# Decoder layer on one core: VectorE takes a unit of exponentials in chunks 1 and 16 too, the accumulators are summed inside a unit, and their transposes are spread over three chunks

## The reference: what is computed

```python
x = layernorm(x + distance_attention(x, U))         # softmax(-squared distances) @ x
q, k, v = x @ Wq + bq, ctx @ Wk + bk, ctx @ Wv + bv # 16 heads of 8
attn = softmax(q k^T / sqrt(8)) ; out = attn @ v    # 1024 x 6404 for each of 16 heads
x = layernorm(x + out @ Wo + bo)
x = layernorm(x + ffn(x))                           # gated, with fake-quantised weights and inputs
```

## Time and profile before

| | |
|---|---|
| median of 3 runs | 824.02 us (822.88 to 824.13) |
| profiled execution | 824.79 us, of which the span from first to last instruction is 823.1 us |
| busy share of the span | ACT 89%, PE 86%, DVE 74%, POOL 21% |
| cross attention | from about 103 us to about 776 us of the span |
| one phase | 83.6 us |

### The profile page before, as it was taken

One profiled execution on the slowest core, in us unless ns is written; L12 is line 12 of the kernel. 1 busy time (PEld: TensorE's weight loads), 2 busy tenths in 40 slices (PEclk: granted clock), 3 DMA queues, 4 the chain that ended last, 5 costly groups with the idle time before them and its releaser, 6 DMA issues.

```text
span 823.1 us, 36628 instructions
## 1 busy us (share of the span) xinstructions
PE 705.3 (86%) x15084; PEld 316.5 (38%) x15084; DVE 609.9 (74%) x1712; ACT 733.5 (89%) x650; POOL 170.7 (21%) x304
## 2 busy tenths in 40 slices
PE   6996679999999999998999898999999999989841
PEld 3444424443444344434443444334433443344321
DVE  3519756886888688858886888778877886788666
ACT  2436788999999999999999999999999999999741
POOL 2501511221222122212221222122211221122100
PEclk9999989999999999999999999999999999999975
DMA  3303521111111111111111111111111111111000
GB/s 106 83 22 115 169 86 48 44 41 41 43 38 37 43 46 36 37 44 44 40 35 42 45 40 35 41 45 41 35 40 46 41 35 40 41 36 35 5 1 25
DMA packets 36607, 38.36 MB, mean 47 GB/s; under 512 B 8430, under 2 KB 35088, under 8 KB 36512
## 3 DMA queue, kind: packets, MB, share of 16 engines
q1 hardware_dynamic: 35644, 36.59, 15.5%
q10 hardware_dynamic: 868, 0.48, 0.2%
HBM read 30.15 MB, written 6.42 MB: 44 GB/s over the span
## 4 chain that ended last, share of the span: by engine, by line
ACT 54%; issue 26%; PE 9%; DVE 4%; SPq 3%; DMA 1%; ACTq 1%; POOL 1%; POOLq 0%; DVEq 0%
ACT probs L714 53%; SPq L291 2%; PE ps L1224 2%; PE ps L1210 2%; PE ps L1325 1%; DMA k_parts_dram<-k_parts 1%; ACTq L727 1%; DMA q_parts_dram<-q_parts 1%; DVE stats L780 1%; POOL k_parts L545 1%; PE ps L1173 1%; DVE probs L1104 0%; PE ps L1152 0%; SPq L312 0%; ACTq L712 0%
## 5 line engine op out<-in xcount | busy, mean ns | idle before, releaser
L714 ACT ACTIVATE probs<-ps 128x1536 f32<-128x1536 f32 (+1 forms) x536 | 669.5, 1393 | 6.4 <-PE ps L1295 6.4
L1325 PE MATMUL ps<-probs,v_op 64*9 64x512 f32 (+1 forms) x8256 | 524.7, 499 | 3.8 <-DMA k_op<-k_parts_dram 3.8
L1295 PE MATMUL ps<-q_op,k_op 59*32 59x512 bf16 x6432 | 335.4, 383 | 64.6 <-ACT probs L714 61.7
L1295 PEld LDWEIGHTS ps<-q_op,k_op 59*32 59x32 bf16 x6432 | 103.6, 90 | 349.7 <-issue 258.7
L964 DVE TENSOR_SCALAR e_t<-ps 128x256 f32<-128x256 f32 x240 | 90.7, 419 | 146.9 <-PE ps L1295 146.9
L1325 PEld LDWEIGHTS ps<-probs,v_op 64*9 64x9 f32 x8256 | 172.4, 87 | 66.6 <-issue 10.1
L592 POOL TENSOR_SCALAR e_pow<-e_t 128x512 int32<-128x512 int16 x120 | 74.4, 620 | 356.4 <-DVE e_t L964 356.4
L585 POOL COPY v_op<-v_all 128x108 f32<-128x108 f32 x136 | 64.3, 473 | 175.1 <-PE ps L1325 174.4
L992 DVE SCALAR_TENSOR_TENSOR e_f<-e_f,e_pow 128x256 f32<-128x256 f32 x240 | 98.6, 449 | 0.0
L986 DVE SCALAR_TENSOR_TENSOR e_f<-e_u,e_f 128x256 f32<-128x256 f32 x240 | 90.4, 418 | 0.0
L981 DVE SCALAR_TENSOR_TENSOR e_u<-e_f 128x256 f32<-128x256 f32 x240 | 90.2, 417 | 0.2
(11 more groups left out here) (179 smaller groups left out, 262.8 us busy)
## 6 DMA issues: line engine op xcount, KB each, us to landing
k_op<-k_parts_dram SPq DMA_DIRECT2D x544, 36.0 KB
k_parts_dram<-k_parts SPq DMA_DIRECT2D x17, 288.0 KB, 3.1
k_op<-k_parts_dram SPq DMA_DIRECT2D x272, 12.0 KB
ctx_nat<-in_ctx_dram SPq DMA_DIRECT2D x16, 192.0 KB, 2.9
q_op<-q_parts_dram SPq DMA_DIRECT2D x32, 48.0 KB
q_parts_dram<-q_parts SPq DMA_DIRECT2D x2, 384.0 KB, 4.3
x_nat<-in_x_dram SPq DMA_DIRECT2D x1, 512.0 KB, 3.7
o_t<-att_rows SPq DMA_DIRECT2D x28, 16.0 KB
```

The costliest lines, as they stand in the source:

```text
L714: act.activation(probs[:, b % NP].rearrange("p u t -> p (u t)")[:, 0:columns], ps[:, bank:bank + BU, :].rearrange("p u t -> p (u t)")[:, 0 ...
L1295: return pe.matmul(ps[a:a + P // G, bank, :], k_op[W2 * r:W2 * r + KR, kslot, i, P * j + a:P * j + a + P // G], q_op[W2 * r:W2 * r + KR, q ...
L1325: last = pe.matmul(ps[32 * k:32 * k + DH + 1, ACC[h], a:b], v_op[W2 * h:W2 * h + W2, slot, j, (DH + 1) * k:(DH + 1) * (k + 1)], probs[W2 * ...
```

## The change

ScalarE's instruction for block s = 2 gets 1024 columns in chunks 1 and 16 as well, and VectorE and GpSimd do a unit there: 17 units in a phase for 15. `power` is cut in two, `factors` (the two stages of the polynomial that need no power of two) and `power` (the last two). `add_acc` stands between `factors` and `power` of chunk 0, where it stood between `take` and `power`. The four instructions that turn and normalise the accumulators stood behind the unit of chunk 0; now `turn_acc` stands behind the unit of chunk 1, `normalise_acc` behind that of chunk 2, `turn_rows` behind that of chunk 3. On TensorE the values of chunk 16 move one step later in chunk 0, from s = 0, 1, 2 to s = 1, 2, 3, with a wait for the unit of chunk 16 in front of the last; and step s = 1 of chunk 0 waits until the unit of chunk 16 has been taken out of its bank.

```diff
-E_UNITS = NC - 2
+E_UNITS = NC
...
-            return ph * E_UNITS + max(c - 1, 0) + 1
+            return ph * E_UNITS + c + 1
...
-                    if c != 1 and c < NC - 1:
-                        powers(ph, c)
+                    powers(ph, c)
...
                 for s in range(BPC, 2 * BPC):
-                    exponentials(f + s, f + (s + 1 + AHEAD))
-                with act.Fori(0, E_UNITS // 2) as r:
+                    exponentials(f + s, f + (s + 1 + AHEAD), shared(s - BPC))
+                with act.Fori(0, (NC - 3) // 2) as r:
...
                 for s in range((NC - 1) * BPC, BPP):
-                    exponentials(f + s, f + (s + 1 + AHEAD))
+                    exponentials(f + s, f + (s + 1 + AHEAD), shared(s - (NC - 1) * BPC))
...
             for ph in range(PHASES):
-                take(ph, 0)
-                if ph:
-                    add_acc(ph - 1)
-                power(ph, 0)
-                if ph:
-                    turn_acc()
...
-                for c in range(2, NC - 1):
+                for c in range(NC):
                     take(ph, c)
+                    factors(ph, c)
+                    if ph and c == 0:
+                        add_acc(ph - 1)
                     power(ph, c)
+                    if ph and c == 1:
+                        turn_acc()
+                    if ph and c == 2:
+                        normalise_acc()
+                    if ph and c == 3:
+                        turn_rows(ph)
...
+                    if s == 1 and c == 0 and ph:
+
+                        pe.wait_ge(e_step, E_STEPS * (e_count(ph - 1, NC - 1) - 1) + E_TAKEN)
...
                     if c == 0:
-                        if s < CT:
-                            values(slot, f - LAST_BPC, s, True, count=2 if s == 1 else 1)
+                        if s == 3:
+                            pe.wait_ge(e_probs, 2 * e_count(ph - 1, NC - 1))
+                        if s:
+                            values(slot, f - LAST_BPC, s - 1, True, count=2 if s == 2 else 1)
...
             for j in range(CT):
                 pe.wait_ge(probs_ready, BLOCKS + min(j + 1, 2))
+                if j == CT - 1:
+                    pe.wait_ge(e_probs, 2 * E_UNITS * PHASES)
```

More of the change, by code:

```diff
@@ L972, in take, with factors @@
                                              ).then_inc(e_step, 1)
-            def power(ph, c):
-                block = ph * BPP + c * BPC + E_BLOCK
+            def factors(ph, c):
                 done = E_STEPS * (e_count(ph, c) - 1)
-                a, b, d, e = EXP2
+                a, d = EXP2[0], EXP2[2]
                 for n, cols in enumerate(halves):
@@ L988, in power @@
                                              ).then_inc(e_step, 1)
+            def power(ph, c):
+                block = ph * BPP + c * BPC + E_BLOCK
+                done = E_STEPS * (e_count(ph, c) - 1)
+                b, e = EXP2[1], EXP2[3]
                 for n, cols in enumerate(halves):
@@ L1004, in turn_acc, with normalise_acc @@
                 acc_chain.step(dve.reciprocal(att_rden[:], acc_t[:, :, DH]))
+            def normalise_acc():
                 acc_chain.step(dve.tensor_tensor(
@@ L1008, in turn_acc, with turn_rows @@
                             [list(att_rden[:].ap[0]), [1, HQ // R], [0, DH]]), ALU.mult))
+            def turn_rows(ph):
+                if ph > 1:
+                    dve.wait_ge(o_written, 16 * G * (ph - 1))
+                dve.transpose(att_rows[:], acc_t[:].rearrange("p n d -> p (n d)")).then_inc(att_ready, 1)
             for ph in range(PHASES):
-                take(ph, 0)
-                if ph:
-                    add_acc(ph - 1)
-                power(ph, 0)
-                if ph:
-                    turn_acc()
-                    if ph > 1:
-                        dve.wait_ge(o_written, 16 * G * (ph - 1))
-                    dve.transpose(att_rows[:], acc_t[:].rearrange("p n d -> p (n d)")).then_inc(att_ready, 1)
-                for c in range(2, NC - 1):
+                for c in range(NC):
                     take(ph, c)
+                    factors(ph, c)
+                    if ph and c == 0:
+                        add_acc(ph - 1)
                     power(ph, c)
+                    if ph and c == 1:
[4 more added lines that the diff above has]
+                        turn_rows(ph)
             dve.wait_ge(x1_bo_ready, 1)
```

## The result

The changed kernel takes **835.06 us**, the median of 6 runs (830.86 to 841.76), beside 824.08 us for the kernel before (6 runs, 822.88 to 826.18): a ratio of 1.013, 95% interval 1.0084 to 1.0175. Forecast were 826.1 us and a range up to 828.4. The profiled execution took 836.24 us with a span of 834.5. So the kernel is slower, and by some 9 us more than I had worked out.

A forecast was written before the change was run, and what follows sets the result against it. ScalarE was taken to set the pace. Seven changes of phase at +0.16 us, +1.1, plus 0.95 in the tail gave 2.05 us on 824.02: 826.1 us, range 822.6 to 828.4.

The forecast's parts named there:

- a unit given away is worth 0.43 us: ScalarE's shortened block: 0.915 us against 1.345 for a full one; two units give 0.86 us per change of phase.
- the new unit of chunk 16 lies too close ahead of that of chunk 0: VectorE at a change of phase: units three blocks, 3.6 us, apart, while one takes 4.02 to 4.09 us.
- 1.02 us late in chunk 1: ScalarE's exponentials of s = 3 end at 12.46 instead of 11.44 us; bounds 0.78 to 1.13.
- The walk: Step-by-step timing of a change of phase from VectorE's chunk 16 unit; add_acc done at 8.1 to 8.2 us.
- No wait in chunk 0's steps: Expected sign: chunk 0's new waits cost nothing, being covered by VectorE's own lateness.
- TensorE's wait at some 1.4 us: Expected sign: TensorE's first values in chunk 1 wait for add_acc, once in each phase from 1 on, seven times.
- -0.86 + 1.02 = +0.16 ... Seven: +1.1 us: Net per change of phase, ScalarE's gain against its lateness, bounds -0.08 to +0.27; over seven, -0.6 to +1.9 us.
- no term has: Stated way to be wrong: the tail's granted clock falls at another time, which was given no size.
- my rivals: ScalarE keeps pace, 819.0 us (8%); half absorbed, 822.5 (12%); VectorE lengthened more, 828.0 or 830.0 (15%); free tail unit, 825.1.
- the slower one: Rival, 15%: GpSimd's copy holds VectorE 0.28 us in both units ahead of add_acc, 830.0 us; in one, 828.0.
- Spread as they are, they cost nothing: Turning instructions make chunk 2's take some 0.4 us late, within the 0.5 us TensorE's scores are ahead of ScalarE.
- The tail: Behind the last block: VectorE's new unit delays the residual add and statistics, everything behind 0.95 us later (0.9 to 1.1).

The follow-up runs named there:

- filled kernel: Changed kernel with the scores of chunk 1, s = 1 written three times over instead of once, to fill TensorE's idle stretch: 828.39 us, ratio 1.0044.
- Order alone: Kernel before with the two stages of factors put ahead of add_acc in chunk 0, no unit added: 834.62 us, ratio 1.0101.
- Order repaired, units kept: Changed kernel with add_acc put back between take and factors of chunk 0, added units kept: 827.74 us, ratio 1.0035.
- `add_acc` last: Changed kernel with add_acc two stages later, behind all of chunk 0's unit: 840.95 us, ratio 1.0191.
- one extra writing: Kernel before with factors ahead of add_acc and the scores of chunk 1, s = 1 written twice: 832.92 us, ratio 1.0086.
- order-only kernels: Kernel before with factors ahead of add_acc, no unit added: 834.62 us; with chunk 1, s = 1 scores written twice 832.92, three times 827.09.

## Why the prediction was wrong

**What held.** ScalarE sets the pace; a unit given away is worth 0.43 us; the new unit of chunk 16 lies too close ahead of that of chunk 0; the wait for `acc_step` takes the place of the gain, seven times; ScalarE comes out 1.02 us late in chunk 1. The walk gave that 1.02 and the profile shows it to the hundredth, in every phase without a fall and in all of the filled kernel; that it is the hundredth is luck, since my own bounds were 0.78 to 1.13 and single steps were off by 0.1. "No wait in chunk 0's steps" held, and so did the direction. I had put TensorE's wait at some 1.4 us from the moment the values could begin; the profile counts 1.11, from the end of the scores.

**The step that failed** is the size given to the change of phase: "-0.86 + 1.02 = +0.16 ... Seven: +1.1 us". It priced the wait by its length. A wait of TensorE has a second price, put at nothing there: behind it the granted clock may fall to one half, and then the scores that ScalarE is waiting for are the very ones that come at half speed. The rows of before do not show it; TensorE waits 0.40 and 0.73 us for ScalarE in the same steps there, and the clock stays. Measured: 1.69 us in chunk 1 at each fall, 1.55 us by the whole phase, four falls in each of two profiles, 6.2 us. With it, 826.1 becomes 832.3, and 833.2 with the smaller terms below. The last 1.9 us of the measured median are not accounted for; start-up, tail and perhaps the number of falls differ between executions. I named the granted clock only for the tail, as what "no term has", and did not carry the thought to the seven places where my own walk had TensorE standing idle. None of my rivals had it either: the slower one, held copies on VectorE at up to 830.0, named another mechanism, and the units back to back took 4.09 us each, as in my terms.

**Smaller terms.** "Spread as they are, they cost nothing" was off by 0.13 us in chunk 3, 0.9 us over seven phases where no fall covers it. I had chunk 2's take 0.4 late, and it is: unit 1 ends, the transpose and the reciprocal follow, and the take starts at 373.96 behind scores that end at 373.51. What I took for a cover of 0.5 us seems to have been a little less. Whether the turning or the late unit 1 is to blame was not told apart in this kernel. The tail was 0.82 us for 0.95. Without falls the sum would have been 7 x 0.30 + 0.82 = 2.9 us for my 2.05, which is 827.0 and inside the range. The filled kernel, which is that case, came out 4.4 us over the kernel before, so even there 1.5 us are without an account.

**The shares.** Order alone, with no unit added: +10.7 us. The whole change: +11.0. Order repaired, units kept: +3.8. The shares of units and order do not add up to the whole, because in both kernels falls of the clock do most of the damage. The part of the change that can pay is the unit in chunk 1, whose neighbours lie a full chunk away; the one in chunk 16 gives 0.43 to ScalarE and takes about a microsecond from it.

## What to carry to other kernels

Price a new wait of TensorE twice: by its length, and by what follows if the granted clock falls behind it, at the full-speed and half-speed lengths of the work that comes next; and do so most of all where that work feeds the engine that sets the pace. If the same matmuls take different times in different repetitions of a loop, look at the clock before anything else, and test it by filling the gap with useless work: a kernel that gets faster by computing more has named its cause. And where work is shared out to an engine with room on average, look at the distance between neighbouring pieces, not at the average.

## What the runs showed of the hardware

- An idle stretch of TensorE of 0.56 us ahead of a group of matmuls, at the end of 4.00 us in which it was busy for 2.31, was followed by half the clock in seven of seven places. The kernel before, busy for 2.87 of 4.00 us at the same place with idle stretches of 0.40 and 0.73 us, had no fall. With `add_acc` last it was busy for 1.14 of 4.00 and the clock fell in only two of seven; with one extra writing the last stretch was 0.13 us and it fell in four. So I can't give a rule for it, and the falls' beat of their own, above, may be part of the reason. The Trainium skill, TensorE: Matmul & The Clock Gate, the section "HAM oscillation — how this bites in real kernels", describes long waits for DMA that send the array back to half speed in every tile; here a wait of about half a microsecond for VectorE, on top of the waits that were there, did it.
- A fall costs ScalarE 1.1 to 1.7 us in chunk 1: 7.09 for 5.65 us in the order-only kernels, 7.65 for 5.97 in the changed kernel, 8.42 and 8.93 for 7.31 with `add_acc` last. A whole phase is 1.4 to 1.6 us longer by it.
- 24 extra matmuls of 32 rows by 512 columns at each change of phase, 0.87 us of TensorE's time, left no fall in either kernel that had them. They cost nothing in the changed kernel's idle stretch (chunk 1 at 5.97 us with and without them) and 0.15 us in the shorter one of the order-only kernel (5.80 for 5.65).
